# Three stages of a ten-layer kernel rewritten: linear attention, channel mixing, and the order of the time mixing

## What is computed

```
# rwkv, time mixing: h = layer_norm(x) * g1 + b1, shifted(h) is h one token later
k, v, r = (h*mix + shifted(h)*(1-mix)) @ w_tk, w_tv, w_tr
y = wkv(decay, first, k, v)        # running weighted mean of v, in log space
x = x + sigmoid(r) * y
# rwkv, channel mixing: h = layer_norm(x) * g2 + b2
kk = relu((h*mix_k + shifted(h)*(1-mix_k)) @ w_ck) ** 2     # 128 -> 512
x = x + sigmoid((h*mix_r + shifted(h)*(1-mix_r)) @ w_cr) * (kk @ w_cv)
# light: 16 query heads, 4 key/value heads, 64 wide, chunks of 128 tokens
q, k, v = h @ Wq.T, h @ Wk.T, h @ Wv.T
q, k = q*cos + rotated(q)*sin, k*cos + rotated(k)*sin   # rotated(): halves of 32 swapped, one negated
for each chunk:
    o  = ((q @ k.T) * mask) @ v + (q * q_dec) @ kv
    kv = blk_dec * kv + (k * k_dec).T @ v
x = x + o @ Wo.T
```

## Time and profile before

| | us |
|---|---|
| median of 3 runs (lowest, highest) | 3064.59 (3062.64, 3067.23) |
| the profiled execution, its own time | 3070.64 |
| its span in the trace | 3068.8 |
| PE busy in the span | 2645.9 (86%) |
| DVE busy | 2060.6 (67%) |
| POOL busy | 1557.8 (51%) |
| ACT busy | 1377.7 (45%) |

### The profile page before, as it was taken

The page is one execution under the profiler, slowest core; times in us unless marked ns, Lnnn a source line. Parts: engine busy times, 40 slices in busy tenths (PEclk is TensorE's granted clock), DMA queues, the critical chain, the costliest instruction groups (busy, mean ns, idle before and its releaser), DMA issues. The chain is left out here.

```text
span 3068.8 us, 43579 instructions
## 1 busy us (share of the span) xinstructions
PE 2645.9 (86%) x13512; PEld 1769.3 (58%) x13512; DVE 2060.6 (67%) x4666; ACT 1377.7 (45%) x2157; POOL 1557.8 (51%) x1449
## 2 busy tenths in 40 slices
PE   4476996997789699788898869999799999979999
PEld 3354664665656466445454447777455555547777
DVE  6755764775577377556555657777577777767777
ACT  4433453444445344211111135556366666645555
POOL 5734644443275444254545435554666666635554
PEclk8688797998889799899999989999799999979999
DMA  1000210000021000100000010000000000010000
GB/s 34 0 12 5 50 35 25 1 1 17 5 52 33 24 1 1 54 1 1 1 0 0 0 41 1 1 1 1 11 1 1 1 0 0 0 42 8 4 8 11
DMA packets 36517, 37.09 MB, mean 12 GB/s; under 512 B 12536, under 2 KB 25208, under 8 KB 36088
## 3 DMA queue, kind: packets, MB, share of 16 engines
q1 hardware_dynamic: 36344, 34.95, 4.2%
HBM read 20.11 MB, written 2.10 MB: 7 GB/s over the span
## 5 line engine op out<-in xcount | busy, mean ns | idle before, releaser
L1903 DVE TENSOR_REDUCE l_diffneg_max<-psum 128x1 fp32r<-128x512 f32 x536 | 364.2, 688 | 119.5 <-PE psum L1656 113.9
L3851 POOL TENSOR_TENSOR l_moe1sc<-l_moe1s,l_moe1bcs 128x512 f32<-128x512 f32 x192 | 263.5, 1384 | 202.0 <-ACT l_moe1s L3562 191.7
L1823 ACT ACTIVATE l_diffweights<-psum 128x1024 f32<-128x1024 f32 x256 | 262.3, 1025 | 155.5 <-PE psum L1683 153.4
L3730 DVE TENSOR_TENSOR l_moe1g<-l_moe1sc,psum 128x512 f32<-128x512 f32 x256 | 174.7, 683 | 134.1 <-POOL l_moe1sc L3851 74.2
L3737 DVE TENSOR_TENSOR l_moe1g_lo<-l_moe1g,l_moe1g_hi 128x512 fp32r<-128x512 f32 x256 | 232.7, 910 | 0.0
L149 POOL TENSOR_TENSOR settled<-powers 128x1 f32<-128x1 f32 x116 | 33.7, 290 | 391.0 <-DVE l_moe1mv L3624 95.3
L1656 PE MATMUL psum<-l_diffkz,l_diffQ 128*128 128x512 f32 x536 | 229.9, 429 | 0.3 <-DVE l_diffneg_max L1903 0.2
L478 PE MATMUL psum<-l_moe1h_hi,l_moe1w_hi 128*128 128x512 f32 x512 | 206.4, 403 | 17.5 <-DVE l_moe1g L3730 12.8
L1234 DVE TENSOR_REDUCE l_attn0neg_max<-psum 128x1 fp32r<-128x512 f32 x256 | 167.2, 684 | 54.2 <-PE psum L977 51.5
L479 PE MATMUL psum<-l_moe1h_hi,l_moe1w_lo 128*128 128x512 f32 x512 | 203.3, 397 | 0.0
L480 PE MATMUL psum<-l_moe1h_lo,l_moe1w_hi 128*128 128x512 f32 x512 | 203.2, 397 | 0.0
(11 more groups left out here) (475 smaller groups left out, 7355.2 us busy)
## 6 DMA issues: line engine op xcount, KB each, us to landing
l_attn0Q<-l_attn0q_hi SPq DMA_DIRECT2D x128, 64.0 KB, 2.0
l_moe1w_raw<-in_moe_w SPq DMA_DIRECT2D x24, 256.0 KB, 5.4
l_attn0Q<-l_attn0q_lo SPq DMA_DIRECT2D x64, 64.0 KB, 2.0
l_moe0w_raw<-in_moe_w SPq DMA_DIRECT2D x24, 128.0 KB, 2.5
x<-in_x SPq DMA_DIRECT2D x8, 256.0 KB, 4.5
out<-x SPq DMA_DIRECT2D x8, 256.0 KB, 2.3
x<-in_light_w SPq DMA_DIRECT2D x3, 512.0 KB, 4.4
l_attn0Q<-l_attn0max_rows SPq DMA_DIRECT2D x64, 2.0 KB, 1.7
```

The costliest lines, as they stand in the source:

```text
L1823: nc.scalar.activation(weights[:, tt, 2 * pair:2 * pair + 2, :], ps[:, S[m % 2]:S[m % 2] + 2, :], ACT.Exp, scale=SCALE).then_inc(act_exp.s ...
L1903: nc.vector.tensor_reduce(neg_max[:, n % 2, st, row:row + 1], ps[:, bank_of(("max", n, b)), :], AXX, ALU.max, negate=True).then_inc(vec_ma ...
L3730: v.tensor_tensor(g[:, n % G_RING, h, :], (s if is_shared(n) else sc)[:, n % 2, h, :], ps[:, H3[(n * HT + h) % 3], :], ALU.mult).then_inc( ...
L3851: nc.gpsimd.tensor_tensor(sc[:, n % 2, h, :], s[:, n % 2, h, :], bcs[:, n % 2, :], ALU.mult).then_inc(pool_sc.sem, pool_sc.step("sc", h))
```

## The change

**Linear attention.** It is written out over all 16 groups, without a loop. Each unit is projected once: 3 matmuls instead of 6, into the bank EVEN or ODD. The swapped copy is made from that bank: four ACT copies of 32 partitions each, from quarter n to quarter n xor 1 (`swap`; in the first group DVE makes two of the five). DVE multiplies the PSUM bank by cos and the swapped copy, now in SBUF, by sin. o is copied whole by ACT; Wo takes 4 fp32 matmuls a group, and both groups of a sequence add up in one bank. The bank R ring is gone: keys turned and key_values share one bank (KV), so `keys_turned(g+1)` waits for the state of chunk 2. The loaded weights are half as wide, in four pieces.

**Channel mixing.** Also written out. The mixed tokens are made once (ACT `now`, DVE `mix`, ACT hi, DVE lo), so that a ck tile takes 3 matmuls instead of 6; DVE squares (relu from SBUF times PSUM), and w_cv takes one fp32 matmul a tile. cr keeps its 6.

**Time mixing.** ACT's `head_hi(s+2)` stands ahead of `logarithms(s)`; DVE's statistics and z stand earlier; POOL's `token_scale` stands ahead of `distance`; the split of the weights stands behind the first and second tokens.

```diff
 # light_block
-                for user, c in zip(banks_of_unit(n, gp, unit), cols):
-                    b = ring(t, i, user)
-                    product(nc, ps[:, b, :], w_hi[:, c:c + P], w_lo[:, c:c + P], head.hi[:, par, :], head.lo[:, par, :]
-                            ).then_inc(pe_seq.sem, pe_seq.step("proj", *user[2:]))
+                c = LI_K + gp * P if unit == "k" else LI_Q + (gp * PER_KV + int(unit[1])) * P
+                product(nc, ps[:, BANK[unit], :], w_hi[:, c:c + P], w_lo[:, c:c + P], head.hi[:, j % 2, :], head.lo[:, j % 2, :]
+                        ).then_inc(pe_proj.sem, pe_proj.step(unit))
...
+        def swap_parts(g, unit):
+            place = (g * len(UNITS) + UNITS.index(unit)) % 2
+            for n in range(4):
+                to, frm = slice(32 * n, 32 * n + 32), slice(32 * (n ^ 1), 32 * (n ^ 1) + 32)
+                yield swapped[to, place, :], ps[frm, BANK[unit], :]
...
+            def keys_turned(g):
+                pe_kt.start()
+                wait(t, pool_sum, g, "k")
+                wait(t, vec_state, g - 1, 2)
...
+                for u in range(PER_KV):
+                    c = (gp * PER_KV + u) * P
+                    ins = nc.tensor.matmul(ps[:, MISC, :], weights_in.out[:, c:c + P], o[:, u, :],
+                                           start=(gp == 0 and u == 0), stop=(gp == 1 and u == PER_KV - 1))
...
+            def by_sin(g, unit):
+                if unit == "k":
+                    vec_sin.start()
+                wait_swap(d, g, unit)
+                v.tensor_tensor(turned[:, place(g, unit), 1, :], swapped[:, place(g, unit), :], sin[:, :], ALU.mult
...
 # channel_mix_block
-                nc.scalar.activation(sq_hi[:, n % RING, :], sq[:, n % 2, :], ACT.Copy).then_inc(act.sem, act.step("sq_hi", n))
+                v.scalar_tensor_tensor(mix[:, :], head.full[:, 0:T], w.rest_k, now[:, :], ALU.mult, ALU.add
+                                       ).then_inc(vec_mix.sem, vec_mix.step("mix"))
...
+                v.tensor_tensor(square[:, n % RING, :], relu[:, n % 2, :], ps[:, H[n % 3], :], ALU.mult).then_inc(vec_sq.sem, vec_sq.step(f))
...
 # time_mix_block, ScalarE
+                if real(s + 2):
+                    head_hi(s + 2)
+                    if s + 2 == 0:
+                        weights_in.scalar_part(a)
                 if real(s):
                     logarithms(s)
-                if real(s + 2):
-                    head_hi(s + 2)
```

More of the change, by code:

```diff
@@ L2403, in _, with swap @@
-            head.start()
-            head.scalar_hi(a, 0, 0)
-            weights_in.scalar_part(a)
-            rest(None, 2, 0)
-            with a.Fori(0, PAIRS) as i:
-                pair_of_sequences(i)
+            def swap(g, unit):
+                if unit == "k" and g > 0:
+                    act_swap.start()
+                wait(a, vec_cos, g, unit)
+                wait(a, vec_sin, *unit_before(g, unit, 2))
+                for to, frm in swap_parts(g, unit):
+                    ins = copy(to, frm)
+                if g == 0:
+                    ins.then_inc(act_first, 1)
+                else:
+                    ins.then_inc(act_swap.sem, act_swap.step(unit))
@@ new lines, in tail @@
+            def tail(j):
+                vec_tail.start()
+                wait(d, pe_tail, j, "tail")
+                at = slice(j * T, (j + 1) * T)
+                v.tensor_tensor(core.x[:, at], core.x[:, at], ps[:, MISC, :], ALU.add).then_inc(vec_tail.sem, vec_tail.step("tail"))
+            head.statistics(d, 0)
+            weights_in.vector_part(d, 0)
+            head.vector_z(d, 0)
+            for n in range(1, len(LI_PIECES) - 1):
+                weights_in.vector_part(d, n)
+            head.low(d, 0)
@@ new lines, in channel_mix_block @@
+        fixed = core_semaphore(nc, name + "_pads_cleared")
+        now, mix = sb("now", [P, T]), sb("mix", [P, T])
+        m_hi, m_lo = sb("mix_hi", [P, 2, T], F32R), sb("mix_lo", [P, 2, T], F32R)
+        relu = sb("relu", [P, 2, T])
+        square, gate, out_sb = sb("square", [P, RING, T]), sb("gate", [P, 2, T]), sb("out_sb", [P, 2, T])
+        block = ctx.enter_context(nc.Block())
+        real = lambda j: 0 <= j < NSEQ
+        SLOTS = range(-1, NSEQ)
+        wait = Ahead.wait
+        @block.sync
@@ new lines, in _, with tokens_now @@
+            for of in (head.act_hi, act_now, act_mhi, act_gate, act_relu):
+                of.credit(a)
+            act = nc.scalar.activation
+            a.wait_ge(w.vectors, 64)
+            a.wait_ge(fixed, 3)
+            def tokens_now(j):
+                act_now.start()
+                wait(a, head.pe_tr, j, "tr")
+                wait(a, vec_mix, j - 1, "mix")
+                act(now[:, :], ps[:, TR, :], ACT.Identity, bias=w.bias_k, scale=w.gain_k).then_inc(act_now.sem, act_now.step("now"))
@@ new lines, in rectified @@
+            def rectified(j, f):
+                if f == 0:
+                    act_relu.start()
+                n = FT * j + f
+                wait(a, pe_ck, j, f)
+                wait(a, vec_sq, *divmod(n - 2, FT))
+                act(relu[:, n % 2, :], ps[:, H[n % 3], :], ACT.Relu).then_inc(act_relu.sem, act_relu.step(f))
+            a.wait_ge(w.turned, 4)
+            tokens_now(0)
+            head_high(0)
+            mix_high(0)
+            w.scalar_part(a)
+            for s in range(NSEQ):
+                rectified(s, 0)
+                gated(s)
+                rectified(s, 1)
+                if real(s + 1):
+                    tokens_now(s + 1)
+                    head_high(s + 1)
+                rectified(s, 2)
+                if real(s + 1):
+                    mix_high(s + 1)
+                rectified(s, 3)
```

1171 lines of the change are left out of this document (609 added, 562 removed).

## The result

The changed kernel takes 2954.05 us (median of 4 runs, 2950.61 to 2955.98) against 3065.57 before (median of 4, 3062.64 to 3067.23): a ratio of 0.9636, 95% interval 0.9619 to 0.9653. The forecast was 2945, its range 2880 to 3005. The gain is 111.5 us, the forecast's sum 119.

A forecast was written before the change was run, and what follows sets the result against it. Linear attention and channel mixing were taken as bound mostly by PE, time mixing by a DVE, ACT and POOL loop. Gains of 78 + 34 + 7 = 119 us from 3070.6 gave 2951.6, or 2945.6 as a median; range 2880 to 3005.

The forecast's parts named there:

- What bounds the stages: Linear attention and channel mixing bound mostly by PE, with some waits; time mixing by a loop through DVE, ACT and POOL.
- PE's pieces: Linear attention: PE's operations priced from the trace, giving a new load of 22.2 us a group against 30.85 now.
- Sine products: Linear attention, DVE: products with sin, both inputs now in SBUF, contend with POOL; 1.5 us more a group taken.
- The first group's wait: Linear attention: in a sequence's first group PE idles 6.5 us before turning the keys, waiting for DVE's z and state.
- the walk: Groups traced engine by engine: linear attention 51.9 us a sequence, 54.0 with the clock; channel mixing 11.5, 12.3 with it.
- The linear attention's sum: Seven sequences at 54.0 instead of 61.7 us, the last sequence 18.7 less, start 5 earlier: 78 us less.
- Channel mixing: A sequence falls from 16.1 to 12.3 us, cr waiting for the low part; the stage gives 34 us.
- Time mixing: Kept no longer waits for the statistics: 1.2 us in each of six slots; the stage gives 7 us.
- B: Linear attention: z hidden or meeting idle POOL, PE's work sets the pace; 48 us a sequence, 2890 in all; chance 0.22.
- C: Contention and swaps set the pace; linear attention 59 us a sequence, channel mixing 13.5, 2995 in all; chance 0.23.
- D: Linear attention: waits before the turned keys hold PE at the lower clock, making the kernel slower, 3110; chance 0.05.
- The sign against B: PE busy over 95% of the linear attention stage would show the forecast wrong and this rival right.

The follow-up runs named there:

- e7: Changed kernel with the linear attention's output product on operands rounded to fp32r, one product each, low parts left out; 2960.36 us.
- e11: e5 with the output product's operands rounded to fp32r, one product each, low parts left out; 2916.97 us.
- e4: Changed kernel with VectorE's four z instructions in the linear attention moved behind the state of chunk 2 and the cosine product of q3; 2931.71 us.
- e5: Changed kernel with VectorE's state of chunk 2 ahead of the mask of chunk 2 in every group, and z behind the cosine product of q3; 2916.54 us.
- e10: e5 with, in channel mixing, VectorE's low part ahead of the fourth tile's square and the last sequence's sum behind that square; 2900.92 us.
- e8: Changed kernel with the time mixing's VectorE statistics back behind less_v, GpSimd's new order kept; 2972.79 us.
- e9: Changed kernel with GpSimd's old order in the time mixing (distance and received ahead of token_scale), early statistics kept; 2956.00 us, one run.
- e12: Changed kernel with ScalarE's old order in the time mixing (logarithms ahead of head_hi); 2950.87 us, one run.
- e6: Changed kernel with each swap made by one copy of 128 partitions in place of four of 32, the rotation's exchange left out; 2918.08 us.
- e2: Changed kernel with the channel mixing of the kernel before, all else as changed; 3005.11 us.

## Why the prediction was right

The forecast was right in direction, size and mechanism; its median is 9 us low. Point by point:

- **What bounds the stages.** Right: time mixing's loop, the channel round and the linear attention gave 7.9, 34.6 and 64.7 us when taken back.
- **PE's pieces.** Right: four fp32 products 3.59 to 3.60 as in the earlier trace rows; PE's 385.44 us in 16 groups is 24.1 a group with what runs at the low level, 22.2 forecast. That this isn't the pace was right, and e7 and e11 show it for both kinds of group; what I then expected of e7 and e11 was not.
- **ACT.** About 240 us forecast for the stage, 249.44 measured; a swap of four copies in 2.39 us (0.60 a copy), where 2.1 was taken from two of the earlier trace rows. 32 partitions bought nothing, as read from 4.
- **Sine products.** 80 took 64.8 us, 0.810 each, against 0.686 with PSUM: 9.9 us in all, 1.2 a sequence, where I had taken 3. 65 of them took 0.7 us with GpSimd idle, 15 took 1.3 and overlapped it for 60% of that. So the contention is there, at less than half the price that I gave it. The Trainium skill, "GPSIMD Engine Reference", section "8. Key points", has GpSimd contend with VectorE's instructions of two SBUF inputs; the trace after agrees.
- **The first group's wait.** Forecast 6.5 us from the walk, 4 to 7 as the sign; measured 6.04 in every steady first group and 0.82 to 0.84 in second ones, as named. z took 2.89, not 3.62. The low clock behind the wait cost 2.08 - 1.13 and 1.97 - 1.08, and in the turn 0.87 - 0.52: 2.2 us, where 2.1 had been added. e4 and e5 show that the wait is what it was called: with DVE's order changed it goes to 3.23 and 0.19, and the time falls with it.
- **The walk.** From one key_values to the next: first group 30.3 us (28.6 and the clock forecast), second 24.3 (23.3). 54.63 against 54.0.
- **The linear attention's sum** is the term that was mis-sized, 66.8 for 78. Between the first and the seventh turn six sequences gave 40.4 us, 6.7 each and not 7.7: 0.6 of it is the period, the rest that these six had averaged 61.46 before, not 61.7, and 54.72 after. From the first product to the first turn the gain was 5.6 instead of 7.7, with the five swaps in a row that no step of mine counted (the first turned keys come 23.6 us after the first product, 12.4 before). The last sequence gave 16.5 for 18.7, the start 4.3 for 5.
- **Channel mixing.** Right: 12.53 a round for 12.3, the first product 4.0 us sooner for 3.7. That cr waits for the low part at the end of DVE's chain was a step of the walk; e10 shows it as the bound. The chain without the clock was 11.5 in the walk and is 11.4 in the two rounds at 1.00; the 0.8 for the clock was about 1.6 in four rounds (one of which also waits 0.4 longer) and nothing in two.
- **Time mixing.** Right, 7.7 for 7, and by the step named (e8 against e9 and e12).
- **Rivals.** B fell in e7 and e11. C had a real part, since the swaps cost 3.5 us a sequence in e6, but the forecast's walk contained them. D: the low clock did come behind the wait, but for 2.2 us a sequence; PEclk of the stage fell from 0.93 to 0.91 and not under 0.8. The sign against B, PE busy over 95%, stayed away (83%).
- **Luck.** The three stages add to 109.1 for 119, and untouched code gave 10.9 in the two profiled executions. The medians compare 111.5 with 119. The spans differ by 120.0; the 8.5 between that and 111.5 are how the two profiled executions lie to their medians, 5.1 above it before and 3.4 below it after. Within the period two misses met: the first group came out 0.4 us under its forecast and the second 1.0 over.

What stays open: which loop holds e5 at 48.9 us a sequence. It isn't PE's work (e11); the swaps are the nearest suspect, since most of PE's new waits in e11 are for them, but e6 wasn't repeated on e5.

## What to carry to other kernels

When work is taken from the engine that was the bound, look at once for what each other engine has queued ahead of the one result that the bound engine waits for: here VectorE's order alone, two lines moved, gave 37 us more, as much as the whole channel mixing's rewrite. An operation for a later sequence (z, statistics, a sum to be stored) belongs behind the state that this group needs; but statistics that start another engine's chain belong ahead (e8: 19 us). A walk of one group with measured durations, engine by engine, gave the period within 1.2%, where PE's load alone would have been wrong by 19%.

## What the runs showed of the hardware that I had not expected

The same attention code behind the channel mixing took 199.8 us in the changed kernel, 203.4 in e4 and 207.0 in e2; the rows are their tables of busy times in that order:

```profile
253.15:452.93 199.78, 176.31 (x1392) 109.63 (x1392) 127.83 (x253) 91.09 (x116) 116.08 (x85) 0.91 0.15 35
```

```profile
253.17:456.53 203.36, 180.32 (x1392) 112.94 (x1392) 127.81 (x253) 91.14 (x116) 116.02 (x85) 0.89 0.14 34
```

```profile
288.54:495.52 206.98, 181.97 (x1392) 113.67 (x1392) 127.82 (x253) 91.19 (x116) 116.25 (x85) 0.88 0.14 34
```

DVE, ACT and POOL did the same work to 0.3 us; what differs is the granted clock, 0.91, 0.89 and 0.88, and with it PE's busy time. It is 207.7 at 0.87 in the kernel before. The differential attention, the same code in every run, took 565.3 us in the kernel before, 568.0 in the changed kernel and 576.5 in e7, at 0.96 to 0.97. So 8 to 11 us of a comparison can stand in a stage that nobody touched, 0.3 to 0.4% of the whole. What picks between them was not found: e4 has the same code as the changed kernel up to the attention. A stage's gain is therefore better read from its own stretch, and small ones from several runs.

A wait costs twice: behind the 6.04 us in which PE stood idle, the turned keys, scores and masked products took 4.7 us, where 2.5 would do at the pace of second groups. A shorter wait can cost it too: behind the 3.23 us of e4 scores and masked products took 1.65 us more than at full clock, and behind the waits of 1.9 us in the channel mixing four rounds of six fell to the lower level and two did not. In e7 PE had less work and the stretch a lower clock, 0.88 instead of 0.91, and it was not shorter; e11, with as much work taken out, kept 0.96, so less work alone isn't shown to be the reason.
